# Two edits in a twelve-layer perceiver kernel: the expert lookup's exponentials move to ScalarE, and layer-1 self-attention is issued in another order

## The reference, cut to what matters

```
q, k, v = split(ln(x) @ w_qkv)             # 16 heads of 128
a = softmax(q k^T / sqrt(128))             # per head, 128 x 128
out = (v * column_sum(a)) @ w_o            # 2048 -> 256
```

```
g    = softmax(scores of the 8 chosen)
z    = g * (h . down[expert])              # h: 128 numbers of the token
w    = z * sigmoid(z) = z / (1 + exp(-z))
x   += sum over the 64 chosen of  w * up[expert]
```

## Time and profile before

| | us |
|---|---|
| median of 3 timed runs | 1246.28 |
| their range | 1241.92 to 1247.13 |
| the profiled execution's own time | 1239.18 |
| its span, first to last instruction | 1237.2 |
| TensorE busy | 1073.2 |
| VectorE busy | 692.8 |
| ScalarE busy | 479.4 |
| GpSimd busy | 192.9 |

### The profile page before, as it was taken

The page is one execution under the profiler, slowest core; times in us unless marked ns, Lnnn a source line. Parts: engine busy times, 40 slices in busy tenths (PEclk is TensorE's granted clock), DMA queues, the critical chain, the costliest instruction groups (busy, mean ns, idle before and its releaser), DMA issues.

```text
span 1237.2 us, 22875 instructions
## 1 busy us (share of the span) xinstructions
PE 1073.2 (87%) x9353; PEld 753.3 (61%) x9353; DVE 692.8 (56%) x1534; ACT 479.4 (39%) x1056; POOL 192.9 (16%) x186
## 2 busy tenths in 40 slices
PE   6988899986975999999999997989999471777998
PEld 5866566655754555655555665676666251676886
DVE  4544357772333767665666642637567867555332
ACT  1111147771320344555555674534444230121222
POOL 0003100000001100000000000006886886000000
PEclk9999999997997999999999999999999685978999
DMA  9012300004001200000000002014454443005551
GB/s 382 13 70 84 120 2 2 2 2 165 1 1 58 106 1 1 2 2 2 2 2 2 2 2 84 1 59 111 126 151 125 121 131 89 15 1 212 214 211 54
DMA packets 16183, 84.38 MB, mean 68 GB/s; under 512 B 3153, under 2 KB 3665, under 8 KB 12369
## 3 DMA queue, kind: packets, MB, share of 16 engines
q1 hardware_dynamic: 7888, 57.75, 12.2%
q0 software_dynamic: 8192, 25.17, 7.2%
HBM read 82.65 MB, written 0.26 MB: 67 GB/s over the span
## 4 chain that ended last, share of the span: by engine, by line
PE 67%; DVE 13%; POOL 11%; issue 5%; ACT 3%; DMA 1%; POOLq 0%; SPq 0%; DVEq 0%; ACTq 0%
POOL L2F_rows L2512 8%; PE L2X_bank_ring L1771 7%; PE L2X_bank_ring L1787 6%; PE L2X_bank_read L1801 6%; PE L2X_bank_ring L1710 4%; PE L1X_banks_scores L916 3%; PE L2X_bank_ring L1719 3%; PE L0X_bank_k L457 2%; PE L3F_bank_y L3380 2%; PE L0X_bank_moments L468 2%; PE L3F_bank_gathered L3329 2%; DVE x L2743 2%; PE L3F_bank_gate_up L3340 2%; PE L1X_bank_proj L893 2%; PE L1A_bank_qk L1181 2%
## 5 line engine op out<-in xcount | busy, mean ns | idle before, releaser
L2068 DVE TENSOR_REDUCE L2X_max_parts<-L2X_bank_ring 128x1 f32<-128x512 f32 x256 | 158.3, 683 | 85.7 <-PE L2X_bank_ring L1771 85.7
L1979 ACT ACTIVATE L2X_context_exp<-L2X_bank_ring 128x384 f32<-128x384 f32 (+1 forms) x384 | 144.1, 462 | 62.4 <-PE L2X_bank_ring L1787 59.6
L2512 POOL DMA_INDIRECT L2F_rows<-in_L2F_embed_dram,L2F_expert x128 | 131.6, 1028 | 59.7 <-issue 36.3
L1771 PE MATMUL L2X_bank_ring<-L2X_context_kT,L2X_q_masked 32*128 32x512 f32 x512 | 96.9, 630 | 0.0
L1024 ACT ACTIVATE L1X_probs<-L1X_clipped,L1X_drop,L1X_keep 128x1024 f32<-128x1024 f32 x64 | 77.6, 1237 | 30.7 <-DVE L1X_clipped L1084 23.5
L1084 DVE TENSOR_SCALAR L1X_clipped<-L1X_banks_scores 128x1024 f32<-128x1024 f32 x64 | 75.4, 1219 | 24.6 <-PE L1X_banks_scores L916 22.9
L1787 PE MATMUL L2X_bank_ring<-L2X_q_and_max,L2X_context_kT 32*128 32x384 f32 (+1 forms) x768 | 85.9, 497 | 0.0
L1801 PEld LDWEIGHTS L2X_bank_read<-L2X_context_exp,L2X_context_v_ones 128*32 128x32 f32 x2048 | 50.2, 109 | 43.8 <-issue 33.4
L1801 PE MATMUL L2X_bank_read<-L2X_context_exp,L2X_context_v_ones 128*32 128x128 f32 x2048 | 75.8, 277 | 1.1 <-ACT L2X_context_exp L1979 0.8
L2743 DVE SCALAR_TENSOR_TENSOR x<-L2F_rows,L2F_expert_weight,x 128x256 f32<-128x256 f32 x128 | 62.4, 487 | 4.6
L221 POOL TENSOR_TENSOR L2A_ln_var_inv_sqrt<-L2A_ln_var_plus_eps,consts 128x2 f32<-128x2 f32 x1 | 0.7, 697 | 356.5 <-DVE L2A_ln_var_plus_eps L216 356.5
(11 more groups left out here) (625 smaller groups left out, 2068.8 us busy)
## 6 DMA issues: line engine op xcount, KB each, us to landing
L3F_expert_weights<-in_L3F_experts_dram SPq DMA_DIRECT2D x16, 1280.0 KB, 5.7
L1A_groups<-in_L1A_groups_dram SPq DMA_DIRECT2D x3, 1536.0 KB, 9.6
ctxT<-in_ctxT_dram SPq DMA_DIRECT2D x8, 512.0 KB, 11.1
L0X_tokens<-in_L0X_tokens_dram SPq DMA_DIRECT2D x8, 512.0 KB, 15.3
slot<-in_L1A_dram SPq DMA_DIRECT2D x1, 3584.0 KB, 11.3
slot<-in_L0F_dram SPq DMA_DIRECT2D x1, 3072.0 KB, 11.4
slot<-in_L2A_dram SPq DMA_DIRECT2D x1, 3072.0 KB, 10.9
slot<-in_L2F_dram SPq DMA_DIRECT2D x1, 2476.5 KB, 8.8
```

The lines of the kernel that those rows point to most:

```text
L1771: nc.tensor.matmul(bank[:, :], qm[32 * g:32 * g + 32, b, c, j, :], cT[32 * g:32 * g + 32, s % 3, blk * 512:(blk + 1) * 512], start=True, s ...
L1979: nc.scalar.activation(ex[:, n % NE, g, 0:width(s)], bank_of(s_e, done(n) + g + 1)[:, 0:width(s)], ACT.Exp, scale=SCALE).then_inc(s_e, 1)
L2068: nc.vector.tensor_reduce(parts[:, j, g, blk:blk + 1], bank_of(s_ft, n)[:, :], AX, ALU.max).then_inc(s_ft, 1)
L2512: pool.indirect_dma_start(out=rows[:, r, k, :], out_offset=None, in_=env.dram["L2F_embed"], in_offset=bass.IndirectOffsetOnAxis(idx[:, b, ...
```

## The change

Two independent edits.

- Layer-1 self-attention: a block of values is projected after every second head's queries and keys, not after all four. The column sums alternate between two banks, the second being the bank of `xT`. The output products are split by unit: those of group g - 1 are issued after the scores of group g, and only the last group's are left for the end; all add up in one bank. `head.tensor` now issues 14 idle products ahead of the turning.
- The lookup: the 17 exponentials leave GpSimd. ScalarE computes exp(-z), one behind its part of each of the steps 2, 4, 6, 8, 10, 13, 15, 17, 19, 21, 24, 26, 28 and 30 (pieces 0 to 13), one after the steps, and the last two after `copy_kv(1)`. Each waits for its z. The tile of 1/e and its semaphore go away.

```diff
-    bank_v, bank_c = L.bank("v"), L.bank("colsum")
+    bank_v, bank_c = L.bank("v"), (L.bank("colsum"), bank_x)
...
-            for j in range(HG // 2):
...
+                if h % 2:
+                    project_values(g, h // 2)
...
         def column_sums(u):
             pe.wait_ge(s_pn, u + 1)
-            if u:
-                pe.wait_ge(s_val, u)
-
-            nc.tensor.matmul(bank_c[:, :], env.const("ones"), pn[:, u % 2, :, :].rearrange("p h t -> p (h t)"),
+            if u >= 2:
+                pe.wait_ge(s_val, u - 1)
+            nc.tensor.matmul(bank_c[u % 2][:, :], env.const("ones"), pn[:, u % 2, :, :].rearrange("p h t -> p (h t)"),
                              start=True, stop=True).then_inc(s_c, 1)
 
+        def out_part(u):
+            g, b = units[u]
+            pe.wait_ge(s_val, u + 1)
+            for h in range(g * HG, (g + 1) * HG):
+                i = nc.tensor.matmul(bank_o[:, b * D:(b + 1) * D], val[:, h, b * P:(b + 1) * P], w("w_o")[:, h * D:(h + 1) * D],
+                                     start=(h == 0 and b == 0), stop=(h == 15), skip_group_check=True)
+            if u == len(units) - 1:
+                i.then_inc(s_out, 1)
+
         env.wait_weights(pe, "L1A")
-        head.tensor(pe)
+        head.tensor(pe, 14)
         pe.wait_ge(head.s_xT, 1)
         project_group(0)
         for g in range(NG):
             for b in range(B):
                 scores(g * B + b)
+            if g:
+                for b in range(B):
+                    out_part((g - 1) * B + b)
             if g + 1 < NG:
                 project_group(g + 1)
             for b in range(B):
                 column_sums(g * B + b)
-        pe.wait_ge(s_val, len(units))
         for b in range(B):
-            for h in range(16):
...
+            out_part((NG - 1) * B + b)
...
-    exp_behind = {(m + 2, TOP // 2 - 1): m for m in range(last - 2)}
-    exp_behind.update({(last - 1, TOP - 1): last - 2, (last, TOP - 3): last - 1})
+    exp_step = [2, 4, 6, 8, 10, 13, 15, 17, 19, 21, 24, 26, 28, 30]
...
-        def exp_z(m):
-            _, lo, hi = pieces[m]
-            pool.wait_ge(s_z, m + 1)
-            nc.gpsimd.tensor_tensor(ze[:, m % 3, lo:hi], per_e[:, lo:hi], zz[:, m % 3, lo:hi], ALU.pow).then_inc(s_ze, 1)
...
-                if (n, k) in exp_behind:
-                    exp_z(exp_behind[n, k])
-        for m in range(last, len(pieces)):
-            exp_z(m)
...
+        def exp_z(m):
+            _, lo, hi = pieces[m]
+            act.wait_ge(s_z, m + 1)
+            nc.scalar.activation(ze[:, m % 3, lo:hi], zz[:, m % 3, lo:hi], ACT.Exp, scale=-1.0).then_inc(s_ze, 1)
...
+            if n in exp_step:
+                exp_z(exp_step.index(n))
             if n in (17, 23):
...
+        exp_z(len(exp_step))
         copy_kv(1)
+        for m in range(len(exp_step) + 1, len(pieces)):
+            exp_z(m)
```

More of the change, by code:

```diff
@@ L1183, in project_group, with project_values @@
                 i.then_inc(s_qk, 1)
-            for j in range(HG // 2):
[L1185 to L1192, removed]
+                if h % 2:
+                    project_values(g, h // 2)
+        def project_values(g, j):
+            n = g * (HG // 2) + j
+            if n >= 1:
+                pe.wait_ge(s_vc, n)
+            for h in range(2):
+                for k in range(KC):
+                    i = nc.tensor.matmul(bank_v[:, h * T:(h + 1) * T], wt(g, 2, 2 * j + h, k), head.xT[:, k, :],
+                                         start=(k == 0), stop=(k == KC - 1))
+            i.then_inc(s_v, 1)
         def scores(u):
@@ L1222, in _ @@
                 column_sums(g * B + b)
-        pe.wait_ge(s_val, len(units))
         for b in range(B):
-            for h in range(16):
-                i = nc.tensor.matmul(bank_o[:, b * D:(b + 1) * D], val[:, h, b * P:(b + 1) * P], w("w_o")[:, h * D:(h + 1) * D],
-                                     start=(h == 0), stop=(h == 15))
-        i.then_inc(s_out, 1)
+            out_part((NG - 1) * B + b)
     @block.gpsimd
@@ L1294, in scale_values @@
             nc.vector.tensor_tensor(val[:, g * HG:(g + 1) * HG, b * P:(b + 1) * P], vT[:, g % 2, :, b * P:(b + 1) * P],
-                                    bank_c[:, :].rearrange("p (h t) -> p h t", h=HG), ALU.mult).then_inc(s_val, 1)
+                                    bank_c[u % 2][:, :].rearrange("p (h t) -> p h t", h=HG), ALU.mult).then_inc(s_val, 1)
         copy_values(0)
@@ L2208, in layer_L2F @@
     ze, wt = L.sb("z_exp", [P, 3, TOP]), L.sb("expert_weight", [P, 3, TOP])
-    per_e = L.sb("one_by_e", [P, TOP])
     names = ("dve_chain", "up_done", "up_pre0_ready", "up_pre1_ready", "up_exp_ready", "up_ready", "hT_done", "hT_ready", "h_done",
              "q_done", "q_copied", "sim_done", "sim_copied", "shifted", "softmax_exp", "experts_ready", "z_ready", "z_exp_ready",
-             "rows_used", "h_ready", "base_set")
+             "rows_used", "h_ready")
     (s_chain, s_up, s_pre0, s_pre1, s_ue, s_h1, s_h, s_hT, s_hn, s_q, s_qc, s_sim, s_simc, s_sh, s_se, s_idx, s_z, s_ze,
-     s_used, s_hnc, s_base) = (L.sem(n) for n in names)
+     s_used, s_hnc) = (L.sem(n) for n in names)
     s_rows = [L.sem(f"rows_gathered{r}") for r in range(NR)]
@@ L2488, in _ @@
         head.gpsimd(pool)
-        nc.gpsimd.memset(per_e[:, :], float(np.exp(-1.0))).then_inc(s_base, 1)
         L.clear_previous(pool)
-        def exp_z(m):
-            _, lo, hi = pieces[m]
-            pool.wait_ge(s_z, m + 1)
-            nc.gpsimd.tensor_tensor(ze[:, m % 3, lo:hi], per_e[:, lo:hi], zz[:, m % 3, lo:hi], ALU.pow).then_inc(s_ze, 1)
-        pool.wait_ge(s_base, 1)
         for n, (b, h) in enumerate(chunks):
```

## The result

The changed kernel took 1272.47 us (median of 4, 1269.16 to 1279.43) where the kernel before took 1244.3 (1241.92 to 1247.13) beside it: a ratio of 1.023, 95% interval 1.021 to 1.026. Slower by 28 us, where 34 to 36 less were forecast. The profiled execution took 1272.3 us, with a span of 1270.2.

The account below looks back on a forecast made before the run. TensorE was taken to bound layer-1 self-attention and GpSimd's gathers the lookup. Savings of 16.0 and 20.0 sum to 36.0 us; 1239.18 profiled becomes 1203.2, plus 7.1 for the timed median gives 1210, range 1202 to 1221.

Parts of the forecast that it names:

- Layer 1, 16.0 us: Layer-1 self-attention on TensorE: its end moves from 383.72 to 367.7 us, saving 16.0 us.
- Warming that does not warm: Rival, layer-1 self-attention: idle products end at the low clock, first projection cold as before; 1215 us, chance 0.08.
- The lookup, 20.0 us: Lookup gathers on GpSimd without powers: last gather of chunk 14 ends at 1008.4, before 1028.37; 20.0 us saved.
- The pitch: Lookup: without a power between gathers, a chunk goes from 12.35 to 10.77 us.
- the wait before chunk 8: Lookup: the choice of experts makes VectorE late, so GpSimd stalls 5.4 us for a buffer, where it was 4.85.
- Cost on the path: nothing, covered by 5 us or more: Lookup: exponentials moved to ScalarE are ready 5 us or more before VectorE needs them, adding no time.
- the last steps, 24 to 30: ScalarE in the lookup: these reach exponentials 10 to 13 at about 976 to 1003 us, needed at 981 to 1013.
- 1.58 us a chunk: Lookup: saved when a power leaves GpSimd's queue, 1.68 us plus its 0.18 gap less 0.28 for the next gather.
- Exponentials late on ScalarE: Rival, lookup: last chunks each wait some 2.5 us for ScalarE, the ring passing on about 10; 1220 us, chance 0.12.
- Slower: the steps at the low clock: Rival, lookup: TensorE, stopped four times, stays at 1.2 GHz through steps 15 to 30; 1252.5 us, chance 0.03.
- The two-ports rule that I cited: Lookup: VectorE and GpSimd block each other on shared ports; by it all 20.0 us stands, without it 19.1.

Follow-up runs that it names:

- chip E: Set with prompt increments: the changed kernel, unchanged, run again beside two versions with added pauses; 1206.65 us, ratio 0.972 to the kernel before.
- chips A, C and D: Three sets with late increments; the changed kernel, unchanged, took 1274.33 us on the second and 1278.64 us on the third.
- chip A: Set with late increments: the changed kernel plus 15 GpSimd powers into a tile nobody reads, at the old places; 1237.55 us, ratio 0.992 to the kernel before.
- after_third: The changed kernel, unchanged, run a third time, where increments were late; 1278.64 us (1265.91 to 1279.51).

## Why the prediction was wrong, point by point

**Layer 1, 16.0 us: right in its steps, and a little small.** The first projection starts at 295.91 (297.35 forecast), the groups take 13.86, 17.3, 17.3 and 10.77 us (14.1, 17.55, 17.55, 10.8 forecast), the last output ends at 365.64 (367.7). From `x` to that end it is 75.8 us where it was 93.4, 17.6 less, and it is 75.8 in all thirteen traces with the edit. Of this 1.4 us go again behind the layer, which no term had: from its last output to the lookup's first memset it is 439.3 us with the edit and 437.7 to 438.0 without. Why is open. Alone the edit measured 16.2 and 19.3 us in time, on two chips with late increments. "Warming that does not warm" fell: the idle products took 4.80 us, less than the 5.7 forecast, and the clock is 1.00 behind them.

**The lookup, 20.0 us: right in its steps where increments are prompt, and some 3 us small.** From the lookup's first memset to the root of layer-3 self-attention's norm chip E's trace has 222.0 us, where the two prompt traces of the kernel before have 245.1 and 244.8: 23 us less. The pitch is 10.6 us (862.25 to 872.86; forecast 10.77), the wait before chunk 8 is 6.10 us (5.4), the exponentials take 0.20 us (0.25). In time, chip E's 35.65 us (1242.3 less 1206.65) less 16 leave 19.7, and 1206.65 lies near 1210. That both come out so close is in part luck: by the traces the two edits are worth 39 us, and outside the two stages traces differ by up to 5.8 us ahead of layer-1 self-attention and 2.6 behind the lookup, with either kernel.

**"Cost on the path: nothing, covered by 5 us or more" for the exponentials on ScalarE: this is the step that failed**, in the result and on chips A, C and D. The cover was counted from the trace of before, in which each engine's news reaches the next at once. With late increments the first six exponentials (steps 2 to 13 of ScalarE) start 18 to 28 us after their z is done in the changed kernel's trace; forecast was within 3 us, and on chip E it is 1.1 to 3.5. I had looked for lateness at the last steps, 24 to 30, and at ScalarE's own order; it came in the first chunk, from TensorE and from the release itself.

**What the sum left out** is what the powers did besides computing. The working cost them 1.58 us a chunk and named the work that they delayed, but not who lived in their gaps. On late chips they are the pauses in the gathers in which the other engines' increments get through: powers that compute nothing bring 38 us back (chip A), where the result had lost 47.5 in that stage. So the rival "Exponentials late on ScalarE" named the last link of the chain in the changed kernel, at 10 us where the late kind costs some 66 against chip E, and the cause before it was in no rival. "Slower: the steps at the low clock" is the only rival on the right side (1252.5, 20 us short; its own terms give 1252.3), and by its mechanism that would be luck: the clock falls to 0.60 and 0.50 where TensorE already stands still (845 to 855 us above), and on chip E it is 1.00 from 840 to 865. The low clock is a consequence here. What it adds to the loss was not separated; TensorE is busy 1108.3 us in the result's trace and 1075.0 in chip E's, for the same work.

The two-ports rule that I cited, from the Trainium skill, page "SBUF — State Buffer", section "SBUF: two separate sides", did not decide the result, since no power is left for it to act on. But it shows on the gathers. That page of the Trainium skill also states that whichever of the two starts first holds the ports for its whole instruction. In chip E's trace 13 gathers start ahead of a product of VectorE that they overlap, and all but one (1.13 us) keep their 0.95. Of the 16 that start while the product runs, 14 take 1.19 to 2.00 us, and 15 end 0.8 us behind the product's end. The trace agrees with the page, if issuing a gather counts as a GpSimd instruction that reads SBUF. A product of VectorE's timeline, and two gathers of GpSimd's, one from ahead of it and one from within it:

```profile
853.54 1.22 DVE L2735 TENSOR_TENSOR L2F_rows<-L2F_rows,L2F_h 128x1024 f32<-128x1024 f32 x1 [6.45 <-DMA L2F_rows<-in_L2F_embed_dram,L2F_expert]
...
853.00 0.95 POOL L2513 DMA_INDIRECT L2F_rows<-in_L2F_embed_dram,L2F_expert  x1 [0.30 <-issue]
854.25 1.33 POOL L2513 DMA_INDIRECT L2F_rows<-in_L2F_embed_dram,L2F_expert  x1 [0.30 <-issue]
```

The time over 0.95 us of all gathers beside products is 6.0 us in the trace of the kernel before and 6.6 in chip E's, so it cancels.

**What stays open** is which part of the chip makes the increments late. Shown is: it goes with the chip, or with its state in that set, since each of the five chips was used in one set; it sets in some 10 us into a run of gathers and ends when they stop; 0.12 us pauses don't help and 1.9 us pauses do; increments are late at the semaphore itself; TensorE stands still even within products that wait for nothing; the records of instructions and of DMA packets are complete (22,927 and 16,182 in the result's trace and in chip E's alike) while three quarters of the gathers' landing records are missing, and with them a fifth of the increments of TensorE, VectorE and ScalarE (410 recorded of 508 made; on chip E 551 of 553).

That last point has a candidate in the Trainium skill, page "NOTIFIC — the notification-queue block", section "7.1 Overflow: three behaviours, one of which stalls the engine": when a queue of records is full, its setting decides whether new records are dropped, the oldest are overwritten, or the engine that makes them is stalled. Dropped increments would fit a queue of the first kind, and engines that stand still with complete instruction records one of the third. Which setting held in these runs isn't on record. Every time here comes with a recorded span and clock, none from an unrecorded execution, so the recording itself can't be excluded as a part of the late kind. Against it: in the 10 us from 710 the late and the prompt trace alike hold over 400 instruction records, more than in the gather stage (353 in the 20 us from 840 on chip E, 113 in the result's), and nothing is late there. What the gather stage has besides is the landings; that these do it was not tested.

## What to carry to other kernels

An instruction between transfers may be a pause that others live on; when it is moved, price the kernel with that engine running without a gap, and look at which engines shared the time. A cover counted in microseconds from one trace holds for that chip: run the kernel on several, and before explaining a difference by an edit, run both kernels in one set with a trace of each. Here that leaves the layer-1 edit alone as the version that beat the kernel before wherever it ran (1229.5 and 1226.5, both with late increments; it was not run where they are prompt), and the joined one as the better where increments are prompt (1206.65) and the worse where they are late (1272 to 1279).

## What the hardware showed that was not expected

- The same program takes 1206.65 us on one chip and 1272 to 1279 on others, each time within 1% on its chip (after_third within 1.1%), while the kernel before takes 1242 to 1247 on all of them. A kernel's slack decides whether a chip's kind is seen.
- In the late kind the gathers themselves don't slow: the median is 0.95 us each and 1.25 us apart in both. In both kinds a gather that starts while VectorE's product of two tiles runs takes up to 2.00 us.
- The increment itself is late, by its own record: 850.19 us for a product that was over at 837.24.
- The landing time of the gathers can be read from the trace only in the prompt kind (min/median/max, changed kernel on chip E): a quick way to tell the kinds.

```profile
DMA to landing us min/median/max: 3.0/3.1/3.2
```
